# Two of the three blocks of M = W1 W2' computed as three one-pass products of split operands

## The reference, cut to what matters

```
hi = h @ W1_w[:384] + emb[a] @ W1_w[384:] + W1_b      (a: adjacency value, 0 or 1)
hj = h @ W2_w[:384] + emb[a] @ W2_w[384:] + W2_b
A  = softmax over j of  sum_e hi*hj, where a != 0
g  = relu((A @ h) @ gcn_w + gcn_b) @ Wo_w + Wo_b
out = layernorm(x + g)
```

## Time and profile before

| | |
|---|---|
| time, median of 3 runs | 372.6 us (372.27 to 373.13) |
| profiled execution, its own time | 373.2 us |
| its span, first to last instruction | 371.3 us |
| mean granted TensorE clock | 0.997 |
| TensorE busy | 364.5 us (98% of the span) |
| VectorE, ScalarE, GpSimd busy | 274.7, 181.5, 145.1 us |
| start of the first projection | 14.29 us |

### The profile page before, as it was taken

How to read it: one execution, slowest core, us unless ns; L and a number is a source line. 1 busy time by engine, 2 the same in 40 slices (tenths; PEclk the granted TensorE clock), 3 DMA queues, 4 the chain that set the end, 5 groups by cost and what they waited for, 6 DMA issues and landing times.

```text
span 371.3 us, 9946 instructions
## 1 busy us (share of the span) xinstructions
PE 364.5 (98%) x3827; PEld 316.8 (85%) x3827; DVE 274.7 (74%) x776; ACT 181.5 (49%) x374; POOL 145.1 (39%) x108
## 2 busy tenths in 40 slices
PE   8999999999999999999999999999999999999994
PEld 5688898988889898888989889898988989898894
DVE  1579778687786868788686777858677786877956
ACT  1576717164372715527272561816347181625574
POOL 1513551716134171513517152261714327141814
PEclk9999999999999999999999999999999999999998
DMA  7996014464443556354365524435553444550033
GB/s 221 352 327 200 24 29 170 158 187 156 139 145 96 173 169 184 116 158 162 89 182 169 179 94 155 160 118 184 169 160 108 129 159 149 171 171 4 2 127 132
DMA packets 43412, 55.48 MB, mean 149 GB/s; under 512 B 10368, under 2 KB 37632, under 8 KB 43392
## 3 DMA queue, kind: packets, MB, share of 16 engines
q1 hardware_dynamic: 42592, 54.44, 46.3%
q10 hardware_dynamic: 800, 0.77, 0.6%
HBM read 42.61 MB, written 12.58 MB: 149 GB/s over the span
## 4 chain that ended last, share of the span: by engine, by line
PE 95%; DMA 2%; DVE 1%; SPq 1%; ACT 0%; issue 0%; POOL 0%
PE banks L471 28%; PE banks L473 27%; PE banks L472 27%; PE banks L531 7%; PE banks L497 7%; DMA xt_sb<-in_x_t_dram 2%; DVE m_lo L920 0%; SPq L398 0%; ACT xt_hi L749 0%; PE banks L616 0%; DVE stats L871 0%; DVE xt_sb L866 0%; SPq L394 0%; POOL rstd L1239 0%; ACT xt_sb L832 0%
## 5 line engine op out<-in xcount | busy, mean ns | idle before, releaser
L1171 POOL TENSOR_TENSOR y_sb<-y_sb,wob_sb 128x1536 f32<-128x1536 f32 x15 | 52.8, 3522 | 88.0 <-DVE y_sb L888 73.9
L783 ACT CAST z_hi<-banks 128x512 fp32r<-128x512 f32 x48 | 26.6, 588 | 96.6 <-PE banks L531 90.8
L866 DVE TENSOR_TENSOR y_sb<-banks,y_sb 128x384 f32<-128x384 f32 x60 | 33.4, 556 | 47.3 <-PE banks L473 43.7
L472 PE MATMUL banks<-wo_lo,hs_hi 128*128 128x384 f32 x180 | 60.5, 336 | 0.0
L471 PE MATMUL banks<-wo_hi,hs_hi 128*128 128x384 f32 x180 | 60.5, 336 | 0.0
L473 PE MATMUL banks<-wo_hi,hs_lo 128*128 128x384 f32 x180 | 60.5, 336 | 0.0
L471 PE MATMUL banks<-z_hi,gcn_hi 128*128 128x512 f32 x144 | 58.3, 405 | 0.0
L471 PE MATMUL banks<-xt_hi,m_hi 128*128 128x512 f32 x144 | 57.1, 397 | 0.5 <-DVE u_sb L922 0.5
L473 PE MATMUL banks<-xt_hi,m_lo 128*128 128x512 f32 x144 | 56.5, 392 | 0.0
L473 PE MATMUL banks<-z_hi,gcn_lo 128*128 128x512 f32 x144 | 56.5, 392 | 0.0
L472 PE MATMUL banks<-z_lo,gcn_hi 128*128 128x512 f32 x144 | 56.1, 390 | 0.0
(11 more groups left out here) (108 smaller groups left out, 614.7 us busy)
## 6 DMA issues: line engine op xcount, KB each, us to landing
x_sb<-in_x_dram SPq DMA_DIRECT2D x16, 768.0 KB, 4.7
xt_sb<-in_x_t_dram SPq DMA_DIRECT2D x15, 768.0 KB, 6.4
y_sb<-in_x_dram SPq DMA_DIRECT2D x15, 768.0 KB, 4.5
out_dram<-y_sb SPq DMA_DIRECT2D x30, 384.0 KB, 2.5
adj_sb<-in_adj_dram SPq DMA_DIRECT2D x32, 64.0 KB, 3.0
xt_sb<-in_x_t_dram SPq DMA_DIRECT2D x2, 384.0 KB, 7.1
xt_sb<-in_x_dram SPq DMA_DIRECT2D x1, 768.0 KB, 6.2
w2t_sb<-in_w_t_dram SPq DMA_DIRECT2D x3, 192.0 KB, 4.6
```

Source lines behind the costliest of these rows:

```text
L472: pe.matmul(acc, a_hi, b_lo, start=False, stop=False)
L783: act.copy(by_graph(z_hi[:, f, :]), mixed(f)).then_inc(zhi, 1)
L866: dve.tensor_tensor(y_home(g, slot)[:, q, :], out_bank(g, q)[:, 0:HID], y_home(g, slot)[:, q, :], ALU.add).then_inc(added, 1)
L1171: pool.tensor_tensor(y_home(g, slot), y_home(g, slot), wob_sb[:].rearrange("p (o n) -> p o n", o=1).to_broadcast([P, PAIRS, HID]), ALU.add ...
```

## The change

Blocks 1 and 2 of the sum for M are no longer plain products: both weights of these blocks are split into high and low parts and multiplied by `three`. Block 0 stays plain. The parts lie in `z_hi` (both parts of `w1t_sb`), `hs_hi` and `hs_lo` (both parts of `w2t_sb` of block 1 and of block 2). The products are 386 columns wide instead of 385: one column of zeros is added beside the column of c2. The eight parts of the weights are placed as follows: the four high parts on ScalarE, ahead of its first `xt_hi`; the two low parts of `w1t_sb` on GpSimd, ahead of L1199; the low part of `w2t_sb` block 1 on VectorE, ahead of the wait for `c_mm`, that of block 2 ahead of L912. The column of c2 is split by two pairs of one-column operations on VectorE, and TensorE waits for them (`c2_lo`) before block 1.

```
-        w2t_sb = sb("w2t_sb", [P, C, HID + 1])
+        w2t_sb = sb("w2t_sb", [P, C, HID + 2])
+        w1_parts = z_hi[:].rearrange("p c t -> p (c t)")
+        w2_parts = hs_hi[:].rearrange("p c t -> p (c t)"), hs_lo[:].rearrange("p c t -> p (c t)")
+        W2 = HID + 2
+        def w1_part(c, low):
+            at = (2 * (c - 1) + low) * HID
+            return w1_parts[:, at:at + HID]
+        def w2_part(c, low):
+            return w2_parts[c - 1][:, low * W2:(low + 1) * W2]
...
 TensorE
-                    mm = pe.matmul(M_BANK[d][:, 0:HID + 1], w1t_sb[:, c, d * P:(d + 1) * P], w2t_sb[:, c, :],
-                                   start=(c == 0), stop=(c == C - 1))
+                    pe.matmul(M_BANK[d][:, 0:W2], w1t_sb[:, c, d * P:(d + 1) * P], w2t_sb[:, c, :],
+                              start=(c == 0), stop=False)
+            def m_parts(c):
+                pe.wait_ge(w1_lo, c)
+                pe.wait_ge(w2_lo, c)
+                for d in range(C):
+                    ds = slice(d * P, (d + 1) * P)
+                    mm = three(M_BANK[d][:, 0:W2], w1_part(c, 0)[:, ds], w1_part(c, 1)[:, ds],
+                               w2_part(c, 0), w2_part(c, 1), False, c == C - 1)
                     if c == C - 1:
                         mm.then_inc(m_mm, 1)
...
-            m_stage(1)
-            m_stage(2)
+            pe.wait_ge(c2_lo, 1)
+            m_parts(1)
+            m_parts(2)
...
 ScalarE
+            for c in range(1, C):
+                act.wait_ge(w12_loaded[c], 32)
+                act.copy(w1_part(c, 0), w1t_sb[:, c, :]).then_inc(w1_hi, 1)
+                act.copy(w2_part(c, 0)[:, 0:HID], w2t_sb[:, c, 0:HID]).then_inc(w2_hi, 1)
             act.wait_ge(xt0_loaded, 16)
...
 VectorE
-            dve.memset(w2t_sb[:, 0, HID:HID + 1], 0.0).then_inc(zero_column, 1)
+            dve.memset(w2t_sb[:, :, HID:HID + 2], 0.0).then_inc(zero_column, 1)
...
+            def low_weights(c):
+                dve.wait_ge(w2_hi, c)
+                dve.tensor_tensor(w2_part(c, 1)[:, 0:HID], w2t_sb[:, c, 0:HID], f32(w2_part(c, 0)[:, 0:HID]),
+                                  ALU.subtract).then_inc(w2_lo, 1)
+            dve.wait_ge(zero_column, 1)
+            for c in range(1, C):
+                for low in range(2):
+                    a = dve.tensor_copy(w2_part(c, low)[:, HID:W2], w2t_sb[:, 0, HID:W2])
+            a.then_inc(zero_parts, 1)
+            low_weights(1)
             dve.wait_ge(c_mm, 1)
...
             dve.wait_ge(c2_ready, 2)
+            dve.wait_ge(zero_parts, 1)
+            for c in range(1, C):
+                a = dve.tensor_copy(w2_part(c, 0)[:, HID:HID + 1], w2t_sb[:, c, HID:HID + 1])
+            a.then_inc(c2_hi, 1)
+            dve.wait_ge(c2_hi, 1)
+            for c in range(1, C):
+                a = dve.tensor_tensor(w2_part(c, 1)[:, HID:HID + 1], w2t_sb[:, c, HID:HID + 1],
+                                      f32(w2_part(c, 0)[:, HID:HID + 1]), ALU.subtract)
+            a.then_inc(c2_lo, 1)
+            low_weights(2)
             dve.wait_ge(c1_ready, 1)
...
 GpSimd
+            for c in range(1, C):
+                pool.wait_ge(w1_hi, c)
+                pool.tensor_tensor(w1_part(c, 1), w1t_sb[:, c, :], f32(w1_part(c, 0)), ALU.subtract).then_inc(w1_lo, 1)
             pool.wait_ge(xhi, 1)
```

More of the change, by code:

```diff
@@ L219, in gnn_layernorm_kernel @@
         zero_column = sem("zero_column")
+        zero_parts = sem("zero_parts")
         attn_zero = sem("attn_zero")
@@ L226, in gnn_layernorm_kernel @@
         c1_ready = sem("c1_ready")
+        w1_hi = sem("w1_hi")
+        w2_hi = sem("w2_hi")
+        w1_lo = sem("w1_lo")
+        w2_lo = sem("w2_lo")
+        c2_hi = sem("c2_hi")
+        c2_lo = sem("c2_lo")
         xt0_hi = sem("xt0_hi")
```

## The result

The changed kernel takes 376.31 us (median of 6 runs, 375.74 to 377.66) against 372.75 us (6 runs, 372.27 to 373.48): a ratio of 1.0093, 95% interval 1.0080 to 1.0107. It is 3.6 us slower; forecast were 1.6 us, with 3.35 us as the price of the first rival.

The account below looks back on a forecast made before the run. TensorE bounds the kernel, so only its first projection's start counts, set by the `xt_sb` load and ScalarE's cast. Late parts gave +1.3 us, with a possible collision +2.0; +1.6 was taken: 372.6 + 1.6 = 374.2 us, range 373.1 to 376.4.

Parts of the forecast that it names:

- the first rival: TensorE's clock falls in the new gap before M's split blocks: 1.75 us on top of 1.6, 376.0 us; chance 0.30.
- the case without a fall: Start of first projection delayed by late parts, clock staying full: +1.0 to +2.5 us, chance 0.45; single number 374.2 us.
- the case that I gave 0.30: TensorE's clock falls in the idle stretch before M's split blocks: +2.5 to +4.5 us, chance 0.30.
- The gain: TensorE's blocks 1 and 2 of M shrink by 0.95 us, but the start moves by 0.1 us at most.
- VectorE held by GpSimd: VectorE's `w2_lo` of block 1 waits for GpSimd's subtraction, ending at 9.96 us; second c2 pair waits until 11.0 us.
- the sum: Waits up to the first projection added up: start at 15.63 us instead of 14.29, +1.3; +1.6 us taken.
- the last collision: VectorE's third `xt_lo` held by GpSimd's L1199 until 14.3 us, first projection at 16.2 us: +2.0 in all.
- its lower end: VectorE is not held by GpSimd, `c2_ready` comes at 9.7 us, first projection starts at 15.0 us: +0.7.
- that rule: GpSimd also blocks float32 copies within SBUF, holding c2's one-column copies until 10.8 us: some +1.9 instead of +1.6 us.
- What is queued behind it: c1 and c2 wait on VectorE behind block 1's low part: `c2_ready` at about 10.2 us, M's split blocks at 11.05.
- The late parts: Split operands of M's blocks 1 and 2 ready late, delaying the first projection: +1.6 us.
- The collision at the third `xt_lo`: VectorE's third `xt_lo` meets GpSimd's L1199 at about 12.3 us; if held until 14.3 us, +2.0 in all.

Follow-up runs that it names:

- a_fill2: Changed kernel with matmuls on zeros (384, 384, 192 columns) filling TensorE's gap before the wait for c2_ready: 374.60 us, ratio 1.0037.
- e_block2: Changed kernel with only block 2 split, block 1 plain, and block 2's VectorE low part behind c2: 373.07 us, ratio 1.0004.
- f_less: Kernel before without block 1 of M (three plain products left out, TensorE waits for its load only): 374.11 us, ratio 1.0030.
- h_pipe: Kernel before, M plain, with casts, subtraction and u_sb copy before the first projection cut into blocks, part of r moved behind its first third: 373.28 us, ratio 1.0011.
- d_unused: Changed kernel with all parts made but unused, blocks 1 and 2 multiplied as plain products: 374.99 us, ratio 1.0066.
- c_nopool: Changed kernel with GpSimd's two weight subtractions replaced by memsets to zero of the same size: 374.23 us, ratio 1.0043.
- b_order: Changed kernel with VectorE's low part of w2t block 1 moved behind c1, c2 and the c2 split: 376.05 us, ratio 1.0078.
- g_hold: Kernel before with VectorE waiting for block 1's weights and writing 1.5 us of zeros ahead of c1 and c2: 373.85 us, ratio 1.0025.

## Why the prediction was right, and where it wasn't

The direction, the place and both mechanisms were right. The time, 376.31 us, lies 0.1 us inside the upper end of the range, and that it lies inside at all is in part luck: the single number, 374.2 us, was the case without a fall, and what happened is the case that I gave 0.30, in all six runs as far as their mean clocks tell (0.991 to 0.995, before 0.996 to 1.00).

- *The gain.* TensorE's work for the two blocks: 18 products, expected 0.174 us apart, are 0.179 us apart in a_fill2 (from 10.90 to 13.77 us in 16 steps). With the first product and the step to L615 the two blocks take 3.41 us, not 3.13, so the work shrinks by 0.67 us and not 0.95. That it counts for next to nothing while the load is the bound was borne out by e_block2 and by the trace of f_less. That it can count for 0.1 us at most is too strong: it was read from one execution, and h_pipe's trace shows one in which M ends last; d_unused against a_fill2 puts the gain at 0.3 us when TensorE is late.
- *ScalarE.* The casts take 0.51 us, and the first `xt_hi` starts at 9.16 us, right behind the fourth of them (8.57 + 0.51 = 9.08 us) and 0.45 us earlier than before. They cost nothing, as said.
- *VectorE held by GpSimd.* Said: `w2_lo` about 1.0 us, the second c2 pair held to the end of `w1_lo`. Found: 1.05 us, and 0.45 instead of 0.15 us. c_nopool prices it at 0.8 us; between the sum (+1.3, without the last collision) and its lower end (+0.7) lay 0.6 us.
- *By the Trainium skill* (page SBUF — State Buffer, section "SBUF: two separate sides") a float32 copy within SBUF would be held as well. Here the one-column casts of c2, from float32 to F32R, ran at 9.3 and 9.4 us in 0.15 us beside GpSimd's subtraction; the measurement decides, and the +0.3 us of that rule didn't come. No run here has a wider copy beside GpSimd's subtraction.
- *What is queued behind it.* c2's products start 2.20 us behind the first cast (said: 2.3), block 1 3.01 us behind it (said: 3.1). The gap before L629 is 2.03 us; said were 2.9, with the load landing 0.8 us later.
- *The late parts.* Said +1.6 us, measured 1.7 us (a_fill2). That they agree so well is luck. The trace has 3.01 us from the first cast to block 1, 3.41 us of products and 1.45 us to the first projection, 7.87 us in all; with the weights at 7.9 us that is a start at 15.8 us, +1.5. The sum without a collision had 3.1, 3.13 and 1.4 us (+1.3), too little for the products, and the 0.3 us that I added were for a collision that cost next to nothing.
- *The collision at the third `xt_lo`* is in the traces of a_fill2 and b_order (three subtractions in 2.73 us instead of 1.08). In a_fill2 the first `m_hi` was ready at 13.55 us and its `m_lo` started at 13.68, so 0.13 us at most was lost there, and TensorE's own queue ran on to the first projection without a gap: it cost next to nothing. In the changed kernel's own trace it isn't there.
- *The step that failed* is the weighing of the first rival: "Against it: each of the two gaps is shorter than 3.2 us." I took the 3.2 us behind the last matmul of the kernel for what a fall needs. The runs show falls with shorter idle stretches: 2.03 and 0.29 us with twelve one-column records between them in the changed kernel, 2.55 us in g_hold. Its price was nearly right: 1.75 us on top was said, 1.7 us is the difference of the medians, 1.5 us that of the traces. The 3.5 us at half clock were 3.4, but a split product takes 0.32 us at half clock, not twice its 0.179. The whole of it, 376.0 us for this case, is 0.3 us from the median. The profiled execution accounts for 3.0 us of the 3.6 (2.2 us later, with the weights 0.8 us earlier); the rest isn't assigned.

Two figures in the weighing are loose. The 887 ns of the warm-up's records are 1.8 times the 487 ns of the plain ones, not twice. And if all of M ran slow, the sum would be 1.6 + 4.5 = 6.1 us, which the case's +2.5 to +4.5 doesn't reach. Neither touches what happened.

What stays open: what decides whether a gap of 2 us makes the clock fall. The changed kernel fell in each run, g_hold (a gap as long, with plain products behind it) in one of 11, d_unused in two of 6. Only two of these falls were seen in a trace, those of the changed kernel and of g_hold; the others are read from mean clocks, and these are a weak sign, because they also hold the half clock behind the last matmul. The runs of f_less have 0.994 to 0.998 and hardly differ in time.

## What to carry to other kernels

Before splitting a product on TensorE into cheaper ones, ask when its operands are ready and what their making is queued ahead of: here 0.67 us of matmuls were saved beside a load, and paid for with a subtraction that stood in front of two tiny ones on which TensorE waited. Make the parts for a block whose turn comes later, and let plain blocks hide them. Read every new idle stretch of TensorE before its first long stream twice, for its length and for the clock that it may cost; a filling of matmuls that is sized by two records for each plain call bought the second back here. And a slack read from one trace of a setup holds for that landing of the loads only.

## What the runs showed of the hardware

- The clock fell to half after TensorE had been idle for 2.03 us, busy with one-column products for 0.5 us and idle for 0.29 us (changed kernel), and after 2.55 us idle and 0.45 us of one-column products (g_hold). Both times it fell only 1.2 and 1.4 us into the stream that followed, and stayed down for 3.4 us of uninterrupted matmuls.
- At half clock split products of 386 columns are 0.32 us apart, at full clock 0.18 us. Twelve records of plain products of 385 columns took 4.08 us at full clock and 5.77 us with the fall in them (g_hold).
- VectorE with two inputs in SBUF is held by GpSimd's subtraction even for a single column (0.86 us for 128 x 1), and in turn between two of GpSimd's (1.36 us for 128 x 384). GpSimd is held too: its second subtraction in the changed kernel took 1.26 us, the first one and both of b_order 1.0 us.
- The landing of the same load of weights differs by 1.0 us between the traces: 4.7 us behind its issue in the changed kernel, 5.5 us in the kernel before, 5.75 us in g_hold.
- One kernel with three plain products less had its last store land 3.6 us behind its issue (f_less, its one trace), against 1.8 to 2.0 us in the eleven others.
